# Combine of a soft mixture-of-experts block turned round: expert outputs stationary, combine weights moving in three f32r products

## What is computed

```
x      = layernorm(x1)                                  # z in the kernel
logits = einsum('bnd,esd->bnes', x, se)                 # 16 experts x 64 slots = 1024 columns
dispatch = softmax over tokens;  combine = softmax over the 1024 slots
slots  = einsum('bnd,bnes->besd', x, dispatch)
eout   = (gelu(slots @ Wg + bg) * (slots @ Wu + bu)) @ Wd + bd      # per expert
out    = layernorm(x1 + einsum('bns,bso->bno', combine, eout))      # the combine stage
```

## Time and profile before

| what | before |
|---|---|
| median of 3 runs | 1312.0 us (1311.98 to 1313.24) |
| profiled execution, its own time | 1315.2 us |
| its span, first to last instruction | 1313.5 us |
| TensorE busy | 1219.5 us, 93% of the span |
| VectorE / ScalarE / GpSimd busy | 814.6 / 681.2 / 450.9 us |
| combine stage on TensorE | 1189.55 to 1300.2 us in the span |
| mean granted TensorE clock | 0.962 of full speed |

### The profile page before, as it was taken

How to read it: one execution, slowest core, us unless ns; L and a number is a source line. 1 busy time by engine, 2 the same in 40 slices (tenths; PEclk the granted TensorE clock), 3 DMA queues, 4 the chain that set the end, 5 groups by cost and what they waited for, 6 DMA issues and landing times.

```text
span 1313.5 us, 19916 instructions
## 1 busy us (share of the span) xinstructions
PE 1219.5 (93%) x7190; PEld 946.7 (72%) x7222; DVE 814.6 (62%) x1318; ACT 681.2 (52%) x1042; POOL 450.9 (34%) x336
## 2 busy tenths in 40 slices
PE   5788999999999999978699999998999999989995
PEld 4555666666666666654588888886788888879885
DVE  3886697878787878751667777764544444432443
ACT  2444565656555565636377777764655555530111
POOL 5554555564655555511100000000544444430000
PEclk9798999999999999987699999999899999999998
DMA  3544363545545453611033333435655555453661
GB/s 123 132 103 108 87 160 91 146 114 126 134 110 142 109 139 89 156 37 65 33 128 113 112 113 113 160 111 159 208 168 161 165 161 165 124 196 105 231 241 48
DMA packets 121791, 170.32 MB, mean 130 GB/s; under 512 B 47025, under 2 KB 76146, under 8 KB 121714
## 3 DMA queue, kind: packets, MB, share of 16 engines
q1 hardware_dynamic: 120818, 168.74, 44.5%
q10 hardware_dynamic: 896, 0.56, 0.1%
HBM read 72.26 MB, written 37.75 MB: 84 GB/s over the span
## 4 chain that ended last, share of the span: by engine, by line
PE 50%; DVE 3%; ACT 2%; issue 1%; DMA 1%; POOL 1%; SPq 0%; ACTq 0%; POOLq 0%; DVEq 0%
PE ring L398 7%; PE ring L399 7%; PE ring L400 7%; PE ring L1490 6%; PE tail L398 3%; PE tail L400 3%; PE tail L399 3%; PE tail L1490 2%; PE ring L1403 2%; PE ring L1396 2%; PE ring L1413 1%; PE tail L1345 1%; PE ring L1334 1%; PE ring L1367 1%; ACT x L806 1%
## 5 line engine op out<-in xcount | busy, mean ns | idle before, releaser
L1050 DVE TENSOR_REDUCE mx<-ring 128x4 f32<-128x512 f32 (+2 forms) x192 | 197.6, 1039 | 81.0 <-PE ring L1319 78.9
L787 ACT ACTIVATE pt<-ring 128x1024 f32<-128x1024 f32 (+1 forms) x192 | 169.4, 883 | 149.6 <-PE ring L1334 138.0
L669 POOL TENSOR_SCALAR_AFFINE_SELECT pt<-pt 128x512 f32<-128x512 f32 x128 | 82.5, 645 | 266.2 <-ACT pt L787 266.2
L1334 PE MATMUL ring<-qks 98*128 98x256 f32 (+3 forms) x512 | 132.1, 362 | 16.3 <-DVE mx L1050 7.5
L1317 PE MATMUL ring<-qks 96*128 96x384 f32 (+3 forms) x512 | 140.8, 364 | 1.9 <-DVE x L1076 0.9
L1334 PEld LDWEIGHTS ring<-qks 98*128 98x128 f32 x512 | 78.0, 196 | 75.7 <-DVE mx L1050 31.7
L694 POOL TENSOR_TENSOR hl<-hid,hh 128x512 fp32r<-128x512 f32 x64 | 82.6, 1302 | 78.2 <-ACT hh L882 78.2
L1345 PE MATMUL tail<-pt,va 128*32 128x512 f32 (+3 forms) x1024 | 99.9, 463 | 8.4 <-POOL pt L669 6.3
L1157 DVE SCALAR_TENSOR_TENSOR hid<-ring,bias_e,gate 128x512 f32<-128x512 f32 x64 | 47.8, 748 | 87.4 <-ACT gate L876 55.4
L1317 PEld LDWEIGHTS ring<-qks 96*128 96x128 f32 x512 | 92.9, 201 | 12.3 <-ACT pt L787 6.3
L680 POOL TENSOR_TENSOR zl<-z,zh 128x1024 fp32r<-128x1024 f32 x8 | 19.1, 2384 | 212.6 <-ACT zh L820 212.6
(11 more groups left out here) (220 smaller groups left out, 3118.5 us busy)
## 6 DMA issues: line engine op xcount, KB each, us to landing
qks<-stg SPq DMA_DIRECT2D x384, 128.0 KB, 2.4
c_dram<-c2s SPq DMA_DIRECT2D x32, 512.0 KB, 4.9
c<-c_dram SPq DMA_DIRECT2D x32, 512.0 KB, 6.0
sl_dram<-sls SPq DMA_DIRECT2D x32, 256.0 KB, 3.4
wg<-in_wg SPq DMA_DIRECT2D x16, 512.0 KB, 5.3
wu<-in_wu SPq DMA_DIRECT2D x16, 512.0 KB, 6.2
wd<-in_wd SPq DMA_DIRECT2D x16, 512.0 KB, 6.9
sl<-sl_dram SPq DMA_DIRECT2D x16, 512.0 KB, 4.4
```

The costliest lines, as they stand in the source:

```text
L669: nc.gpsimd.affine_select(out=m, in_=m, compare_op=ALU.is_ge, fill=0.0, base=0, pattern=[[0, GH], [1, P]], channel_multiplier=-1).then_inc ...
L787: nc.scalar.activation(pt[j % 2][:, h:h + heads, 0:n], heads_of(tile, heads, n), ACT.Exp, scale=SCALE).then_inc(empty, 1)
L1050: nc.vector.tensor_reduce(out=mx[:, g, i, h:h + heads], in_=heads_of(tile, heads, (i + 1) * P), axis=AX.X, op=ALU.max).then_inc(empty, 1)
L1334: last = nc.tensor.matmul(scores[:, h, :], qks[0:KS_ROWS + 2, g, h0 + h, 1, j * P:(j + 1) * P], qks[0:KS_ROWS + 2, g, h0 + h, 0, j * P:T], ...
```

## The change

The product is turned round. `eo` of a batch stands (as 128 slots x 128 channels) and the weights move, 512 tokens wide, so that the sum `acc[i]` has channels on partitions and must be transposed back. Both operands are split per batch into high and low parts, and each product becomes three f32r products (`mm3`). The new steps are:

- ScalarE, `combine_high`: copies 7 of 8 blocks of `eo` of the batch to `eoh[i]`, the four quarters of `c2[i]` to `c2h[i]`, and the last block of `eo`. `drain_out` copies the finished sum to `outT[i]`.
- VectorE, `combine_low`: low parts of quarters 0 and 1 of the weights (`c2l[i]`, in the place of `c2[i]`).
- GpSimd, `combine_low`: low part of 7 blocks of `eo` (`eol[i]`), then of quarters 2 and 3 of the weights, then of the last block.
- TensorE, `combine`: per batch 8 blocks x 2 channel halves x 3 = 48 products of 512 columns. `turn`: 8 transposes of `outT[i]` into `accT[i]`, done for the batch before after the first two blocks of the next one.
- `norm_out` reads `accT[i]`, and SyncE waits for `outT_drained` where it waited for `acc_drained`.

`following(q, i)` is the next batch. Per batch b each engine's order becomes: ScalarE `combine_high(b+1)`, `scale(b-1)`, `drain_out(b)`; VectorE `combine_low(b+1)`, `norm_out(b-1)`.

```diff
+    accT, acc = (ring[0], ring[1]), (ring[2], tail)
@@ SyncE
-                    sp.wait_ge(acc_drained[i], q + 1)
+                    sp.wait_ge(outT_drained[i], q + 1)
@@ GpSimd
+            def combine_low(q, i):
+                b = 2 * q + i
+                if first(b):
+                    pool.wait_ge(hid_low, E * NF)
+                for part, ns in enumerate(EO_PARTS):
+                    if part == 1:
+                        for k in (2, 3):
+                            pool.wait_ge(c2_high, b * 4 + k + 1)
+                            apart(pool)
+                            nc.gpsimd.tensor_tensor(out=c2l[i][:, 2 * k:2 * k + 2, :], in0=c2[i][:, 2 * k:2 * k + 2, :],
+                                                    in1=fp(c2h[i][:, 2 * k:2 * k + 2, :]), op=ALU.subtract).then_inc(c2_low_pool, 1)
+                    pool.wait_ge(eo_high, b * 2 + part + 1)
...
+                    nc.gpsimd.tensor_tensor(out=eol[i][:, ns, :].unsqueeze(2), in0=src, in1=fp(eoh[i][:, ns, :]).unsqueeze(2), op=ALU.subtract).then_inc(eo_low, 1)
@@ ScalarE
+            def combine_high(q, i):
...
+                if not first(q):
+                    act.wait_ge(acc_filled[i], q)
...
+                eo_part(0)
+                for k in range(NS // 2):
+                    act.wait_ge(c2_loaded[i][k], (q + 1) * 16)
+                    apart(act)
+                    nc.scalar.activation(c2h[i][:, 2 * k:2 * k + 2, :], c2[i][:, 2 * k:2 * k + 2, :], ACT.Copy).then_inc(c2_high, 1)
+                eo_part(1)
+            def drain_out(q, i):
+                act.wait_ge(acc_filled[i], q + 1)
+                apart(act)
+                if not first(q):
+                    act.wait_ge(outT_filled[i], q)
+                nc.scalar.activation(outT[i][:, :, :], acc[i][:, :, :], ACT.Copy).then_inc(acc_drained[i], 1)
             def combine_two(q):
-                scale(q, 0)
-                scale(q, 1)
+                for i in range(2):
+                    combine_high(*following(q, i))
+                    if i == 1:
+                        scale(q, 0)
+                    elif not first(q):
+                        scale(q - 1, 1)
+                    drain_out(q, i)
@@ VectorE
+            def combine_low(q, i):
+                b = 2 * q + i
+                for k in range(2):
+                    dve.wait_ge(c2_high, b * 4 + k + 1)
+                    apart(dve)
+                    nc.vector.tensor_tensor(out=c2l[i][:, 2 * k:2 * k + 2, :], in0=c2[i][:, 2 * k:2 * k + 2, :],
+                                            in1=fp(c2h[i][:, 2 * k:2 * k + 2, :]), op=ALU.subtract).then_inc(c2_low, 1)
             def combine_two(q):
-                norm_out(q, 0)
-                norm_out(q, 1)
+                for i in range(2):
+                    combine_low(*following(q, i))
+                    if i == 1:
+                        norm_out(q, 0)
+                    elif not first(q):
+                        norm_out(q - 1, 1)
@@ TensorE
+            def turn(q, i):
+                pe.wait_ge(acc_drained[i], q + 1)
...
+                for t in range(NT):
+                    for d in range(2):
+                        last = nc.tensor.transpose(accT[i][:, t // 2, t % 2 * DO + d * P:t % 2 * DO + (d + 1) * P],
+                                                   outT[i][:, d, t * P:(t + 1) * P], ident[:, :])
+                last.then_inc(outT_filled[i], 1)
+            def combine(q, i):
...
+                for n in range(NS):
+                    if n == 0:
+                        pe.wait_ge(eo_low, 2 * b + 1)
+                    elif n == NS - 1:
+                        pe.wait_ge(eo_low, 2 * b + 2)
+                    if n % 2 == 0:
+                        pe.wait_ge(c2_low if n < 4 else c2_low_pool, 2 * b + n // 2 % 2 + 1)
+                    for d in range(2):
+                        cols = slice(d * P, (d + 1) * P)
+                        last = mm3(acc[i][:, d, :], eoh[i][:, n, cols], eol[i][:, n, cols], c2h[i][:, n, :], c2l[i][:, n, :], n == 0, n == NS - 1)
...
+                    if n == 1:
+                        if i == 1:
+                            turn(q, 0)
+                        elif not first(q):
+                            turn(q - 1, 1)
```

More of the change, by code:

```diff
@@ L290, in block_kernel @@
     y3 = [place(f"y3{i}", [P, NT, C], f32, hidden_at + i * 4 * KB) for i in range(2)]
+    c2l = [place(f"c2l{i}", [P, NS, T], f32r, raw_at[i]) for i in range(2)]
+    c2h = [place(f"c2h{i}", [P, NS, T], f32r, attn_at + o * KB) for i, o in enumerate((52, 92))]
+    eol = [place(f"eol{i}", [P, NS, DO], f32r, attn_at + o * KB) for i, o in enumerate((16, 24))]
+    eoh = [place(f"eoh{i}", [P, NS, DO], f32r, o) for i, o in enumerate((x_at, attn_at + 68 * KB))]
+    outT = [place(f"outT{i}", [P, 2, T], f32, o) for i, o in enumerate((x_at + 8 * KB, attn_at + 76 * KB))]
     st3 = place("st3", [P, NT, 6], f32)
@@ L345, in block_kernel @@
     acc_filled, acc_drained = [sem(f"acc_filled{i}") for i in range(2)], [sem(f"acc_drained{i}") for i in range(2)]
+    c2_high, c2_low, c2_low_pool = sem("c2_high"), sem("c2_low"), sem("c2_low_pool")
+    eo_high, eo_low = sem("eo_high"), sem("eo_low")
+    outT_filled, outT_drained = [sem(f"outT_filled{i}") for i in range(2)], [sem(f"outT_drained{i}") for i in range(2)]
     scale_ready, out_ready = sem("scale_ready"), sem("out_ready")
@@ L917, in scale, with eo_part @@
                 last.then_inc(out_ready, 1)
-            def combine_two(q):
-                scale(q, 0)
-                scale(q, 1)
-            repeat(act, combine_two, B // 2)
+            def combine_high(q, i):
+                b = 2 * q + i
+                def eo_part(part):
+                    ns = EO_PARTS[part]
+                    if first(b):
+                        for k in range(2):
+                            act.wait_ge(eo_placed[k], (NP - 1 + part) * 32)
+                        if part == 0:
+                            act.wait_ge(w_low, 3 * E)
+                            act.wait_ge(w_low_pool, E)
+                    src = eo[:, ns, b:b + 1, :] if isinstance(b, int) else eo[:, ns, bass.ds(b, 1), :]
+                    nc.scalar.activation(eoh[i][:, ns, :].unsqueeze(2), src, ACT.Copy).then_inc(eo_high, 1)
+                if not first(q):
+                    act.wait_ge(acc_filled[i], q)
+                    apart(act)
+                elif i == 0:
+                    act.wait_ge(down_filled, E - 1)
+                else:
+                    act.wait_ge(down_filled, E)
+                eo_part(0)
[6 more added lines that the diff above has]
+                act.wait_ge(acc_filled[i], q + 1)
+                apart(act)
+                if not first(q):
+                    act.wait_ge(outT_filled[i], q)
+                nc.scalar.activation(outT[i][:, :, :], acc[i][:, :, :], ACT.Copy).then_inc(acc_drained[i], 1)
+            def combine_two(q):
+                for i in range(2):
[5 more added lines that the diff above has]
+                    drain_out(q, i)
+            combine_high(0, 0)
+            repeat(act, combine_two, B // 2 - 1)
+            q = B // 2 - 1
+            combine_high(q, 1)
+            scale(q - 1, 1)
+            drain_out(q, 0)
+            scale(q, 0)
+            drain_out(q, 1)
+            scale(q, 1)
         @block.vector
@@ L1191, in _ @@
             expert(NP - 1, 1, False)
+            def combine_low(q, i):
+                b = 2 * q + i
+                for k in range(2):
+                    dve.wait_ge(c2_high, b * 4 + k + 1)
+                    apart(dve)
+                    nc.vector.tensor_tensor(out=c2l[i][:, 2 * k:2 * k + 2, :], in0=c2[i][:, 2 * k:2 * k + 2, :],
+                                            in1=fp(c2h[i][:, 2 * k:2 * k + 2, :]), op=ALU.subtract).then_inc(c2_low, 1)
+            combine_low(0, 0)
             drain_down(NP - 1, 1)
@@ L1202, in clink @@
                     apart(dve)
-                dve.wait_ge(acc_filled[i], q + 1)
+                dve.wait_ge(outT_filled[i], q + 1)
                 dve.wait_ge(x1_loaded[i], (q + 1) * 16)
@@ L1225, in combine_two @@
             def combine_two(q):
-                norm_out(q, 0)
-                norm_out(q, 1)
-            repeat(dve, combine_two, B // 2)
+                for i in range(2):
+                    combine_low(*following(q, i))
+                    if i == 1:
+                        norm_out(q, 0)
+                    elif not first(q):
+                        norm_out(q - 1, 1)
+            repeat(dve, combine_two, B // 2 - 1)
+            q = B // 2 - 1
+            combine_low(q, 1)
+            for done in ((q - 1, 1), (q, 0), (q, 1)):
+                norm_out(*done)
         @block.tensor
@@ new lines, in turn @@
+            def turn(q, i):
+                pe.wait_ge(acc_drained[i], q + 1)
+                if not first(q):
+                    pe.wait_ge(outT_drained[i], q)
+                else:
+                    pe.wait_ge(gu_drained[i], NP * GU_FILLS[i])
```

(22 more changed lines are left out.)

16 lines of the change are left out of this document (12 added, 4 removed).

## The result

The changed kernel takes 1358.87 us (median of 4 runs, 1357.2 to 1359.45) against 1311.99 us before: ratio 1.0354, 95% interval 1.0336 to 1.0372. It is 3.5% slower, 46.9 us; the span of the profiled execution grew from 1313.5 to 1357.2 us, by 43.7. I had forecast slower, 1346.2 us, 34.2 us more. The direction and the mechanism hold; the size was 9.5 us of span and 12.7 us of the median short.

What follows compares the result with a forecast made beforehand. A circle of waits through ScalarE, VectorE and SyncE's queue was to bound the combine, 19.9 us a trip: 1220.2 + 5 x 19.9 + 28.0 = 1347.7, 34.2 us more, so 1346.2 us by the median; range 1328 to 1360.

Steps and rivals of the forecast that it cites:

- TensorE's work: Combine: products and transposes need 12.0 us per batch, 1.8 less than before, worth 7 to 14 us if still the bound.
- The order in which they wait decides: Combine: every engine's work sums to 12.0 us or less per batch, so by sums the change wins; waiting order decides.
- The circle of waits: Combine: drain, high parts, low parts, layernorm, scale, next drain form a loop, one batch per trip, at least 15.7 us.
- rival (1): Combine: TensorE remains the bound, batches 12.03 us apart, 11.8 us less, 1300 us; chance 5%.
- Rival (2): Combine: the circle without the load's wait, trip 15.7 us, 10.7 us more, 1323 us; chance 12%.
- SyncE's queue: Loads for b+2 go out only after storing b-1; ScalarE stands until 6.3 us, lengthening the trip to 19.4 us.
- VectorE beside GpSimd: Layernorm's tiny two-input operations are held by GpSimd subtractions, 0 to 1.1 us per trip, 0.5 taken: trip 19.9 us.
- the last of the signs that I had named: Layernorm: a tiny VectorE operation of 1 us or more in each would show the 0.5 us to be too small.
- The first trip: Combine's start: scale(0) ends at 1218.1, or 1222 if GpSimd holds norm(0)'s tiny chain; 1220.2 taken for drain(1).
- rival 3: Combine: TensorE falls to half clock and bounds, 22.6 us per batch if slow throughout, 1361 us; chance 7%.
- My own case: Combine: circle with load wait and GpSimd hold-ups, trips 17.2 to 21.4 us, 1330 to 1356 us; chance 74%.
- Rival (4): Combine: no change within 0.2%, with trips of about 14.4 us, between rivals (1) and (2); chance 2%.

Runs made afterwards that it cites:

- e11: Changed kernel with layernorm before low parts, transposes after block 0, loads before store, drain before scale, tiny layernorm operands in PSUM: 1306.47 us, ratio 0.9949.
- e2: Changed kernel with SyncE alone reordered, loading the weights for b+2 before it stores b-1: 1359.2 us.
- e1: Changed kernel with ScalarE alone reordered, drain of batch b before scale of b-1: 1347.62 us.
- e12: e11 with SyncE's order set back, loads for b+2 behind the store of b-1: 1318.85 us, ratio 1.0054.
- e7: Changed kernel with all four orders changed: layernorm before low parts, transposes before block 0, loads before store, drain before scale: 1328.72 us, ratio 1.0127.
- e8: As e7, but the transposes of b-1 come after block 0 of batch b: 1331.53 us, ratio 1.0145.
- e6: Changed kernel with layernorm before low parts, transposes before the first block, and loads before the store: 1338.28 us.
- e4: Changed kernel with GpSimd's two subtractions of weight quarters 2 and 3 cut to 8 of 512 columns: 1345.03 us.
- e9: Changed kernel with mean, variance and one operand of the layernorm's tiny operations in PSUM, all orders kept: 1349.06 us.

## Why the prediction was right, and where it was short

- **TensorE's work** was right: the products start 0.23 us apart and a batch of products and transposes is 12.04 us in e11, where I had 12.0. Some 1.5 us of the 1.8 per batch come through: e11's trips are 12.2 to 12.7 us, where the kernel before had 13.8.
- **"The order in which they wait decides"** was right: of the 46.9 us lost, and the 6.8 won in e11, every part was moved by orders and by the place of a few small operands, at the same products and the same subtractions.
- **The circle of waits.** Its terms were right one by one, but its minimum of 15.7 us could not be reached by a better load alone (e2), and the link from scale to drain was not the one that closed it (e1). Against rival (1) I named ScalarE's written order alone. In truth there were several circles: with SyncE's order left the trip stayed at 14.4 us or more (e12), with VectorE's left at 20 to 21 us (e1, e2), and with the orders of all four engines mended but the operands left at 16 us (e7, e8). ScalarE's order was worth about 1 us per trip between e6 and e7; ScalarE's and TensorE's were not set back alone in e11, so whether it needs them is not shown. Rival (2), "the circle without the load's wait", could not have come out as 15.7 for that reason.
- **SyncE's queue**: first quarter needed at 6.3 us, measured 6.2 to 7.4 (6.8 on average), since the first load went out 0.7 to 1.6 us after the drain's start and landed 4.7 to 6.6 us later. With the hops from quarter to quarter the layernorm starts 10.4 us after the drain's start, where I had 9.8: 0.6 of the 1.4 us.
- **VectorE beside GpSimd** is the step that was mis-sized. I took 0.5 us per trip, counting only operations with two inputs in on-chip memory, from 14.3 us of the trip on. Measured, the layernorm takes 8.9 us on average over the five trips, 1.4 above 7.5 and 0.9 above what I allowed: v and r, with one input each, are held too, and they come earlier (v takes 0.70 to 1.37 us in the five trips, r 0.53). This is the last of the signs that I had named, a tiny operation of 1 us or more. e4 and e9 take just this away and bring the trip to 19.5 to 20.8. The Trainium skill, SBUF — State Buffer, section "Who interferes with whom", names `tensor_scalar` among the operations that can enter a two-port mode and so contend for the shared pair; I had used only that section's rule on two inputs, and this case's 1.00 us (v, kernel after) and 2.22 us (r, e6 and e7) agree with it. In which mode they ran no trace shows.
- **The first trip** carried the same fault twice: VectorE's four subtractions of batches 1 and 2 took 12.56 us instead of 4.9, by which norm(0) started 2.8 us later than in my sum, and norm(0) took 11.9 us, 2.3 more than the 7.5 and the 2.1 that I had allowed. I had held up only the layernorm, and not the subtractions: even the upper end of my 0 to 4 us would have covered no more than 1.8 of the 5.0. GpSimd was at work without a pause there, from 1195.5 to 1218.3.
- **TensorE's clock** (rival 3) did fall, to 0.82 on average in a trip. After each idle stretch of 7 us the transposes take 1.97 us instead of 1.03 and the next few products are slow; it is hidden behind the circle, as I had it.
- **The range held in part by luck.** My own case reached up to 1356 us, with trips of 21.4 us that were to come from the load, where they came in larger part from VectorE's hold-ups. The measured 1358.9 lies above that, and inside 1328 to 1360 only because I had widened the range for rivals of which (3), the upper one, did not come.
- **Two sums of the prediction are off.** Rival (4), no change, needs trips of about 13.6 us by my own terms, not 14.4 (1218.1 + 5 x 14.4 + 27.6 = 1317.7, 4.2 more than before). And by the slope of the earlier trace rows GpSimd's last `eo` block costs 0.76 us, not 0.65; it took 0.72 to 0.74. Neither changes the forecast.

## What to carry to other kernels

When work of several engines per step adds up to less than the bound, draw each engine's written order as a chain and look for closed loops before believing the sum; a loop that is cut at one link may close through the next engine's queue, so cuts have to be tried together too, and not only one at a time. A wait that is removed without gain is not proof that it was free: it may keep two other engines apart. And when GpSimd is given large elementwise work beside VectorE, keep the operands of VectorE's short, serial operations in PSUM: from e8 to e11 that alone took the time from 1.0145 to 0.9949 of the kernel before.

## What the runs showed of the hardware that I had not expected

- A `tensor_scalar`, with one input, on 4 elements per partition takes 0.17 us alone and up to 2.22 us beside a GpSimd subtraction (e7), ending with it; with its source in PSUM it takes 0.17 or 0.16 beside the same subtractions (e9). Not every one-input operation is held: in the kernel after, the four bn_stats (1277.78) take 1.40 us and the four bn_aggr (1279.33) 0.38 inside a GpSimd subtraction, as in the kernel before.
- The two engines take turns, instruction by instruction: in e2 two VectorE subtractions of 1.22 us took 7.64 us (4.31 and 3.41) beside GpSimd's. GpSimd pays too: its two subtractions of 2.38 us took 3.38 and 3.40 there, and in e11 its last subtraction of 256 elements takes 1.72 us (at 1229.54 in its timeline) where it took 0.72 to 0.74 elsewhere.
